# Centring each gathered row with a mean carried as a ninth gate column, in one VectorE operation with the add of beta

## What is computed

```python
x = x + xattn(layernorm(x), ctx, ctx, mask, gamma, beta)       # xattn ends in its own layer norm: xhat * gamma + beta
h = layernorm(x)
gate_probs = softmax(h @ w_gate)                               # top 2 of 8 kept, renormalised
g, u = split(h @ w_gate_up[e])                                 # 256 -> 2 x 1024
y = (silu(g) * u) @ w_down[e]                                  # 1024 -> 256
x = x + sum over the two experts of gate_probs[e] * y
```

## Time and profile before

| | |
|---|---|
| median of 3 runs | 455.43 us (455.05 to 455.9) |
| profiled execution | 455.1 us |
| its span, first to last instruction | 453.4 us |
| mean granted clock of TensorE | 0.979 |
| TensorE busy | 429.8 us (95%) |
| VectorE busy | 309.0 us (68%) |
| ScalarE busy | 225.3 us (50%) |
| GpSimd busy | 190.8 us (42%) |

### The profile page before, as it was taken

The page is one execution under the profiler, slowest core; times in us unless marked ns, Lnnn a source line. Parts: engine busy times, 40 slices in busy tenths (PEclk is TensorE's granted clock), DMA queues, the critical chain, the costliest instruction groups (busy, mean ns, idle before and its releaser), DMA issues.

```text
span 453.4 us, 10483 instructions
## 1 busy us (share of the span) xinstructions
PE 429.8 (95%) x2335; PEld 353.0 (78%) x2336; DVE 309.0 (68%) x779; ACT 225.3 (50%) x486; POOL 190.8 (42%) x211
## 2 busy tenths in 40 slices
PE   9998978899999999999999999999999999999980
PEld 5887537788888888888888888888888888888860
DVE  4778978975877577758756568768865678646440
ACT  4787844744554366365533364545634446333330
POOL 5544233454454334544343543435534355343211
PEclk9998699999999999999999999999999999999996
DMA  7773613454355225424531125424541143111120
GB/s 207 203 260 94 220 41 105 144 147 119 83 149 128 35 70 138 141 32 126 160 79 24 24 34 156 134 70 116 128 128 24 24 116 81 35 24 25 13 25 12
DMA packets 28605, 43.87 MB, mean 97 GB/s; under 512 B 2833, under 2 KB 22219, under 8 KB 28587
## 3 DMA queue, kind: packets, MB, share of 16 engines
q1 hardware_dynamic: 20358, 32.95, 23.4%
q0 software_dynamic: 7520, 10.39, 13.7%
q10 hardware_dynamic: 709, 0.32, 0.3%
HBM read 34.02 MB, written 9.64 MB: 96 GB/s over the span
## 4 chain that ended last, share of the span: by engine, by line
PE 85%; DVE 5%; ACT 3%; issue 3%; POOL 1%; DVEq 1%; POOLq 0%; ACTq 0%
PE bank L1308 45%; PE bank L1328 16%; PE bank L1330 8%; PE bank L1318 7%; PE bank L1106 2%; PE bank L1292 2%; PE bank L1175 1%; DVE w L378 1%; PE bank L1152 1%; ACT act L991 1%; ACT place_late L991 1%; PE bank L1138 1%; ACT place_late L995 1%; PE bank L1185 1%; ACT act L995 1%
## 5 line engine op out<-in xcount | busy, mean ns | idle before, releaser
L1308 PE MATMUL bank<-w,tokT_hi 128*128 (+1 forms) x624 | 173.1, 399 | 1.9 <-DVE tokT_lo L831 0.9
L1048 ACT ACTIVATE gated<-bank,row_rstd 128x512 f32<-128x512 f32 x78 | 53.6, 688 | 181.9 <-PE bank L1308 167.9
L1308 PEld LDWEIGHTS bank<-w,tokT_hi 128*128 128x128 f32 x624 | 112.0, 188 | 25.9 <-issue 4.6
L1328 PE MATMUL bank<-w,aT_hi 128*128 (+1 forms) x312 | 119.6, 418 | 1.1 <-DVE y_sb L861 1.1
L840 DVE SCALAR_TENSOR_TENSOR act<-bank,row_rstd,gated 128x512 f32<-128x512 f32 x78 | 58.4, 749 | 83.8 <-ACT gated L1048 83.8
L560 POOL DMA_INDIRECT out<-y_sb,out_i x39 | 62.0, 1589 | 100.4 <-DVE y_sb L861 100.4
L1308 PE MATMUL bank<-w,tokT_lo 128*128 (+1 forms) x312 | 96.5, 390 | 0.0
L1330 PE MATMUL bank<-w,aT_lo 128*128 (+1 forms) x312 | 87.6, 281 | 0.0
L547 POOL TENSOR_TENSOR tok<-tok,beta_b 128x256 f32<-128x256 f32 x38 | 28.8, 758 | 103.8 <-DMA tok<-rows_d,gather_i 103.8
L1308 PEld LDWEIGHTS bank<-w,tokT_lo 128*128 128x128 f32 x312 | 58.6, 188 | 13.0
L1328 PEld LDWEIGHTS bank<-w,aT_hi 128*128 128x128 f32 x312 | 58.8, 188 | 11.9 <-issue 1.3
(11 more groups left out here) (169 smaller groups left out, 413.4 us busy)
## 6 DMA issues: line engine op xcount, KB each, us to landing
raw<-in_L_ffn_w_gate_up SPq DMA_DIRECT2D x32, 512.0 KB
raw<-in_L_ffn_w_down SPq DMA_DIRECT2D x16, 512.0 KB
rows_d<-x_sb SPq DMA_DIRECT2D x8, 264.0 KB, 5.0
x_sb<-in_x SPq DMA_DIRECT2D x8, 256.0 KB, 7.3
out<-x_sb SPq DMA_DIRECT2D x8, 256.0 KB, 4.7
out<-y_sb,out_i POOLq DMA_INDIRECT x39
tok<-rows_d,gather_i POOLq DMA_INDIRECT x38, 3.3
cap<-in_mask_BxSxS_ik SPq DMA_DIRECT2D x1, 462.0 KB, 6.4
```

Of the source, the lines that this page charges most:

```text
L1048: act_e.activation(gated[:, h, :], ps_g[h][:, :], ACT.Silu, scale=row_rstd[:, s:s + 1]).then_inc(gated_set, 1)
L1308: ins = pe.matmul(ps[:, :], tokens_[:, s, k, :], w.rearrange("p a g d -> p (a g) d"), start=(k == 0 and tokens_ is tokT_hi and part == 0), ...
L1328: pe.matmul(ps_y[:, :], aT_hi[:, h, c, :], w.rearrange("p a t d -> p (a t d)"), start=(h == 0 and c == 0), stop=False, skip_group_check=True)
```

## The change

Each row gets a ninth gate column that carries its mean. Its weight is 1/256 in the plain version of `wg_sb`, and the versions for gamma and beta are made from it as for the other eight, so that the column holds the mean of the row with beta. A row in `rows_d` has 265 numbers instead of 264. With the mean there on arrival, VectorE centres a gathered row and adds beta in one operation (`row_centre`), before the statistics; the statistics now give the variance only. GpSimd's `add_beta` and VectorE's L708 and L720 are gone. `row_stats` is cut in two: what leads to `row_var`, and `row_gate` with `other` and `lead`. For block 0, `row_gate` comes after `tok_low`; for blocks 1 and 2 the expert's register is loaded between the two. TensorE's last two spins before block 0, and their wait for the statistics, are gone.

```diff
-    TE = T + E
+    GC = E + 1
+    TE = T + GC
...
-    ROW = D + E
+    ROW = D + GC
...
-        wg_sb = sb("wg_sb", [P, KD, 3, E])
+        wg_sb = sb("wg_sb", [P, KD, 3, GC])
...
+            pool.memset(wg_sb[:, :, 0, E:GC], 1.0 / D).then_inc(mean_col_set, 1)
...
-            def add_beta(b):
-
-                pool.wait_ge(beta_in, 16)
-                pool.wait_ge(tok_in[b % 2], arrival(b, b % 2))
-                pool.tensor_tensor(tok[:, b % 2, 0:D], tok[:, b % 2, 0:D], beta_b[:], ALU.add).then_inc(tok_beta, 1)
...
             row_scale(0)
-            pool.wait_ge(tok_beta, 1)
-            add_beta(1)
             row_scale(1)
             gather(2, gather_i[:, 2:3])
-            add_beta(2)
             row_scale(2)
...
                     gather(b + 2, gather_i[:, b + 2:b + 3])
-                    add_beta(b + 2)
                 add(b - 1)
...
-            def row_stats(b, s, e):
-
-                own = tok[:, s, bass.ds(D + e, 1)]
-                if isinstance(b, int) and b == 0:
-                    dve.wait_ge(tok_in[0], 16)
-                    dve.wait_ge(beta_in, 16)
-                    dve.tensor_tensor(tok[:, 0, 0:D], tok[:, 0, 0:D], beta_b[:], ALU.add).then_inc(tok_beta, 1)
-                dve.wait_ge(tok_beta, b + 1)
+            def row_centre(b, s):
+
+                dve.wait_ge(beta_in, 16)
+                dve.wait_ge(tok_in[s], arrival(b, s))
+                dve.scalar_tensor_tensor(out=tok[:, s, 0:D], in0=tok[:, s, 0:D], scalar=tok[:, s, ROW - 1:ROW], in1=beta_b[:],
+                                         op0=ALU.subtract, op1=ALU.add).then_inc(tok_set, 1)
+
+            def row_stats(b, s):
+
+                dve.wait_ge(tok_set, b + 1)
                 dve.bn_stats(row_stat[:, s, :], tok[:, s, 0:D]).then_inc(row_stats_set, 1)
-                dve.max(top[:, s, :], tok[:, s, D:ROW]).then_inc(top_set, 1)
+                dve.max(top[:, s, :], tok[:, s, D:D + E]).then_inc(top_set, 1)
                 dve.wait_ge(row_stats_set, b + 1)
                 if not isinstance(b, int):
 
                     dve.sem_inc(row_seen, 1)
                 dve.bn_aggr(row_mv[:, s, :], row_stat[:, s, :]).then_inc(row_mv_set, 1)
+                if later(b, 2):
+                    dve.wait_ge(row_rstd_set, b - 1)
+                dve.wait_ge(row_mv_set, b + 1)
+                dve.tensor_scalar(row_var[:, s:s + 1], row_mv[:, s, 1:2], EPS, None, ALU.add).then_inc(row_var_set, 1)
+
+            def row_gate(b, s, e):
+
+                own = tok[:, s, bass.ds(D + e, 1)]
                 dve.wait_ge(top_set, b + 1)
                 dve.tensor_scalar(other[:, s:s + 1], own, top[:, s, 0:1], top[:, s, 1:2], ALU.subtract, ALU.subtract).then_inc(other_set, 1)
-                dve.wait_ge(row_mv_set, b + 1)
-                dve.tensor_scalar(tok[:, s, 0:D], tok[:, s, 0:D], row_mv[:, s, 0:1], None, ALU.subtract).then_inc(tok_set, 1)
-                if later(b, 2):
-                    dve.wait_ge(row_rstd_set, b - 1)
-                dve.tensor_scalar(row_var[:, s:s + 1], row_mv[:, s, 1:2], EPS, None, ALU.add).then_inc(row_var_set, 1)
                 dve.wait_ge(other_set, b + 1)
                 dve.tensor_scalar(lead[:, s:s + 1], own, other[:, s:s + 1], 0.5, ALU.add, ALU.mult).then_inc(lead_set, 1)
...
-            row_stats(0, 0, 0)
+            row_centre(0, 0)
+            row_stats(0, 0)
...
                 if ahead:
-                    row_stats(b + 2, s, expert_of(b + 2))
+                    own = expert_of(b + 2)
+                    row_centre(b + 2, s)
+                    row_stats(b + 2, s)
+                    row_gate(b + 2, s, own)
...
             tok_low(0, 0)
+            row_gate(0, 0, 0)
             split_low(dve, 3)
...
-            row_stats(1, 1, expert_of(1))
+            row_centre(1, 1)
+            row_stats(1, 1)
+            row_gate(1, 1, expert_of(1))
...
-            row_stats(2, 0, expert_of(2))
+            row_centre(2, 0)
+            row_stats(2, 0)
+            row_gate(2, 0, expert_of(2))
...
             pe.wait_ge(tok_in[0], 16)
             spin(2, bank[2])
-            pe.wait_ge(row_stats_set, 1)
-            spin(2, bank[2])
```

More of the change, by code:

```diff
@@ L137, in build @@
         att_scale = sb("att_scale", [P, NT])
-        bias_g = sb("bias_g", [P, E])
-        z = x_gate = x_sb[:, :, D:ROW]
+        bias_g = sb("bias_g", [P, GC])
+        x_gate = x_sb[:, :, D:ROW]
+        z = x_sb[:, :, D:D + E]
         versus = sb("versus", [P, 6, E, E])
@@ L216, in build @@
         ps_ctxT = bank[7][:, 0:2 * KD * T].rearrange("p (b k t) -> p b k t", b=2, k=KD)
-        ps_ctxg = [bank[i][0:T, 320:320 + 2 * E].rearrange("p (b e) -> p b e", e=E) for i in (6, 7, 7, 7)]
+        ps_ctxg = [bank[i][0:T, 320:320 + 2 * GC].rearrange("p (b e) -> p b e", e=GC) for i in (6, 7, 7, 7)]
         ps_colsum = bank[6][:, 0:E]
-        ps_bias = bank[5][:, 0:E]
+        ps_bias = bank[5][:, 0:GC]
         ps_cols = bank[4][:, 0:2 * KD]
@@ L237, in over_t @@
         def over_t(ap, n):
-            return ap.unsqueeze(1).to_broadcast([P, n, E])
+            return ap.unsqueeze(1).to_broadcast([P, n, GC])
         def tiles(b):
@@ L267, in build @@
         centred_set = sem("centred_set")
+        mean_col_set = sem("mean_col_set")
         wg_set = sem("wg_set")
@@ L338, in build @@
         tok_in = [sem(f"tok_in{i}") for i in range(2)]
-        tok_beta = sem("tok_beta")
         row_stats_set = sem("row_stats_set")
@@ L520, in _ @@
             pool.memset(empty[:], 0.0).then_inc(empty_set, 1)
+            pool.wait_ge(mean_col_set, 1)
             pool.wait_ge(centred_set, 1)
-            pool.tensor_copy(ctxT[:, :, :, T:TE], wg_sb[:, :, 0, :].unsqueeze(1).to_broadcast([P, B, KD, E])).then_inc(ctxw_set, 1)
+            pool.tensor_copy(ctxT[:, :, :, T:TE], wg_sb[:, :, 0, :].unsqueeze(1).to_broadcast([P, B, KD, GC])).then_inc(ctxw_set, 1)
             x_rstd(0)
@@ L751, in _ @@
             dve.wait_ge(colsum_ps, 1)
-            dve.scalar_tensor_tensor(out=wg_sb[:, :, 0, :], in0=ps_colsum.unsqueeze(1).to_broadcast([P, KD, E]), scalar=-1.0 / D,
+            dve.scalar_tensor_tensor(out=wg_sb[:, :, 0, 0:E], in0=ps_colsum.unsqueeze(1).to_broadcast([P, KD, E]), scalar=-1.0 / D,
                                      in1=w_gate_sb[:], op0=ALU.mult, op1=ALU.add).then_inc(centred_set, 1)
@@ L757, in _ @@
             dve.wait_ge(cols_ps, 1)
+            dve.wait_ge(mean_col_set, 1)
             dve.scalar_tensor_tensor(out=wg_sb[:, :, 1, :], in0=wg_sb[:, :, 0, :], scalar=16.0,
-                                     in1=ps_cols[:, 0:KD].unsqueeze(2).to_broadcast([P, KD, E]), op0=ALU.mult, op1=ALU.mult).then_inc(wg_set, 1)
-            dve.tensor_tensor(wg_sb[:, :, 2, :], wg_sb[:, :, 0, :], ps_cols[:, KD:2 * KD].unsqueeze(2).to_broadcast([P, KD, E]),
+                                     in1=ps_cols[:, 0:KD].unsqueeze(2).to_broadcast([P, KD, GC]), op0=ALU.mult, op1=ALU.mult).then_inc(wg_set, 1)
+            dve.tensor_tensor(wg_sb[:, :, 2, :], wg_sb[:, :, 0, :], ps_cols[:, KD:2 * KD].unsqueeze(2).to_broadcast([P, KD, GC]),
                               ALU.mult).then_inc(wg_set, 1)
```

## The result

The changed kernel takes 467.73 us (median; 465.83 to 468.27) against 455.66 us for the kernel before in the same rounds: ratio 1.025, 95% interval 1.0235 to 1.0266. A second measurement gave 467.87 and 455.95, ratio 1.0255 (1.024 to 1.027). It is slower by 12 us, where I had forecast 6.3 us and a range that ended at 466.

What follows compares the result with a forecast made beforehand. TensorE's matmuls are 85% of the chain, so VectorE counts only where TensorE waits for it. 455.1 + 6.0 (loop) + 0.4 (split blocks ahead) + 0.3 (start) = 461.8, stated as 461.7 us; range 457 to 466.

Steps and rivals of the forecast that it cites:

- the rule: Loop: stall before a block is a (0.2, back edge 0.5) plus d, less the previous stall; +6.0 us over six runs.
- The centring's price: VectorE, ahead of the statistics: the new operation costs 0.50 with its step plus 0.03 for a second wait.
- the reckoning from 134.00: VectorE, statistics to split in a split block: split at 1.70 against 1.68 before, so the lost subtract frees nothing.
- d: Delay of aT_lo in the loop's split blocks: 0.53 us, between 0.42 and 0.62.
- Its own sign for a wrong size: The size is wrong if the centring on VectorE takes something other than 0.45 to 0.5 us.
- The blocks ahead of these: The two split blocks ahead of the loop have more room: +0.4 us (0 to 0.8).
- The start: Start of the expert part: -0.5 at row 0's split, -0.5 at L885, row 1 +0.1, row 2 +1.2; +0.3 us.
- rival 4: Loop: the centring waits for GpSimd's scatter (L560), d = 1.0, 467.7 us; half that wait 464.5; chance 0.06.
- Rival 1: Loop: idle spells come from something other than aT_lo, so only the start counts; no change, 455.4 us; chance 0.09.
- rival 2: Loop loses nothing and row 2's load at the start stays hidden: faster, 454.3 us; chance 0.07.
- rival 3: Loop: centring overlaps register work, or other and lead close up; d 0.15 to 0.4, 457 to 459.5 us; chance 0.06.
- the rest: Ninth column on matmuls, GpSimd memset, 4 bytes more per gathered row: 0, at most 0.2 us together.

Runs made afterwards that it cites:

- experiment 6: Changed kernel with TensorE's two register loads for the loop's even block issued ahead of down(b-1, 1): 464.52 us beside 456.08 for the kernel before.
- experiment 5: Changed kernel with other put back ahead of row_var in the loop, centring kept, no subtract: 463.53 us, ratio 1.0147 to the kernel before.
- experiment 2: Kernel before plus the centring's operation alone, written to a dead tile ahead of the statistics from row 3 on: 462.90 us, ratio 1.0149.
- experiment 4: Changed kernel with GpSimd, not VectorE, centring and adding beta from row 3 on: 460.97 us, ratio 1.0096 to the kernel before.
- experiment 1: Kernel before with only the ninth gate column, rows of 265 numbers and the earlier GpSimd memset: 455.20 us beside 456.08, ratio 0.9982.
- experiment 10: Changed kernel with seven TensorE spins before its wait for block 1's act, 466.62 us; kernel before with that wait lengthened, 457.55; changed kernel remeasured, 467.87.
- experiment 3: Changed kernel with a 128 x 256 subtract to a dead tile between other and lead from row 3 on: 466.12 us beside 456.08.
- experiment 9: Changed kernel with expert loads of rows 1 and 2 ahead of tok_low, 466.67 us; behind queued splits, 466.18; first placement with statistics behind aT_lo, 456.43.

## Why the prediction was wrong in size

- **The bound and the mechanism were right.** The loss is in the idle spells before the first gate and up half of a block; they follow aT_lo in split blocks by the same 2.4 and 2.75 us; hoisting TensorE's loads moves them as the rule says (experiment 6). The Trainium skill's rule from "Perfetto Trace Analysis", "Per-instruction lifecycle: what the profiler-reported window actually captures", that the sequencer passes an instruction with an unmet semaphore, was misapplied in the prediction. The page says so of instructions that an engine executes; where the sequencer itself executes the instruction, the same section has the sequencer wait. In the trace it is the register operation of L1328 that carries the wait for aT_lo, so on TensorE page and trace agree. On VectorE they don't: lead is an engine's instruction, and yet the branch behind it starts only when lead's semaphore is met, 128.2 against 128.15 (experiment 5). The measurement decides.
- **The centring's price was right**: forecast 0.53, measured 0.52.
- **The step that failed is the reckoning from 134.00**: "row_var at 0.80, other at 0.95, lead at 1.26, split at 1.70". Measured: row_var 0.86, other 1.03, split 1.95. Other was a little off, but the fault was to step from lead to the split by the 0.43 of the earlier trace rows. That 0.43 isn't a cost of its own: the split stands 0.65 behind the end of other, because the sequencer reaches the branch only then. By that, my own 0.95 would have given 0.95 + 0.27 + 0.65 = 1.87, and d = 0.72. With the measured other it is d = 0.84 (0.52 and 0.3, experiments 2, 4 and 5): what the prediction put at nothing is the second part. Its own sign for a wrong size, a centring outside 0.45 to 0.5, did not fire: that took 0.49, and the size was wrong all the same.
- **The rule** with d = 0.84 gives +9.7 us for the six runs of three, where I had +6.0; the trace, from y_low at 115.50 to the last (113.65 before), has +8.8. The spells with the back edge alone reach 1.25, not the 1.34 of the rule. Against experiment 1's kernel, whose rows are as wide, it has +9.4: the shorter clean blocks had hidden 0.7 of the loss. The blocks ahead of these took +0.9 instead of +0.4.
- **The start** cost 1.0 instead of 0.3: 0.24 came in with the attention part (the first centring is at 63.23, the add before at 62.99), which is within the spread of the traces (62.99 to 64.55). L890 was right: 0.17 us, where L885 took 0.72, and 0.71 to 0.72 in each kernel that keeps GpSimd's add there. The Trainium skill's "SBUF — State Buffer", section "SBUF: two separate sides", agrees in that the two engines exclude each other; L885 has one input, so it doesn't bear out the clause on two inputs that rival 4 leans on. Row 1's load cost 0.5 net, not 0.1, row 2 1.4, not 1.2.
- **The clock** was in no step. The median stands 1.9 above the profiled execution, and the mean clocks of seven of nine executions are those of traces with the second stretch (experiment 10); that this is the 1.9 us is argued, not shown. Sum: 9.6 + 1.0 + 0.1 = 10.7 in the traces, 12.1 in the medians.
- **Rival 4** had priced 467.7, with d = 1.0, but its mechanism is not there: the 35 centrings from 97 us on take 483 to 492 ns, none waits for GpSimd's scatter. That it hits the median is luck. **Rivals 1 to 3** are out by the trace. Of "the rest", experiment 1 shows the ninth column to be free.

## What to carry to other kernels

When an in-order engine has small operations with waits in front of a branch, find the last wait that its sequencer must pass, and count the branch from there; the gap between the last operation and what follows the branch isn't a price. Moving an operation that waits ahead of one that is waited for costs the difference, even if no work is added. And when a change takes a dependence away (here the centring's on the statistics), look at what can now be moved off the critical place: the same instructions in another order turned 12 us lost into 4 gained.

## What was new of the hardware

- The split starts 0.64 to 0.69 us after other ends, in the kernel before and five others, with a 0.34 us operation queued in between or not (experiments 2 to 5).
- Two register loads ahead of VectorE's tok_low took 1.38 us in the open; one behind a queued split of 1.2 us showed nothing (experiment 9).
- In six traces TensorE worked for 3.4 us at half clock, which loses at most 1.7 us, behind a wait of 2.4 to 3.0 us; in five other traces with such a wait it didn't. With spins in the wait no execution of five had a mean clock under 0.978 (experiment 10).
- With rows of 265 numbers in place of 264, clean blocks were 0.02 to 0.03 us shorter (experiment 1); the cause is open.
